# Attention over grouped heads beside a quantized feed-forward: two runs of transposes and one score product are put into one row inside a projection

## The reference

```python
q = (x @ wq).reshape(B, S, 32, 128)      # 32 query heads
k = (x @ wk).reshape(B, S, 8, 128)       # 8 key and value heads, 4 query heads to each
v = (x @ wv).reshape(B, S, 8, 128)
q, k = rope(q), rope(k)
scores = einsum('bqhgd,bshd->bhgqs', qg, k) * 128 ** -0.5
allowed = (j <= i) & (j > i - 128)       # a sliding window of 128 positions
attn = softmax(where(allowed, scores, most_negative))
out = einsum('bhgqs,bshd->bqhgd', attn, v).reshape(B, S, 32 * 128) @ wo
h = silu(xn @ W1.T) * (xn @ W3.T);  ffn = h @ W2.T   # W1, W3, W2 from packed 4-bit numbers
```

## Time and profile before

| | |
|---|---|
| median of 3 runs | 802.33 us (802.15 to 803.08) |
| profiled execution | 802.26 us |
| its span, first to last instruction | 800.4 us |
| granted TensorE clock over the span | 1.000 of full speed |
| TensorE matrix products busy | 796.0 us (99%) |
| VectorE, ScalarE, GpSimd busy | 567.4, 428.5, 475.2 us |

### The profile page before, as it was taken

The page is one execution under the profiler, slowest core; times in us unless marked ns, Lnnn a source line. Parts: engine busy times, 40 slices in busy tenths (PEclk is TensorE's granted clock), DMA queues, the critical chain, the costliest instruction groups (busy, mean ns, idle before and its releaser), DMA issues.

```text
span 800.4 us, 13468 instructions
## 1 busy us (share of the span) xinstructions
PE 796.0 (99%) x3966; PEld 672.4 (84%) x3966; DVE 567.4 (71%) x1634; ACT 428.5 (54%) x1104; POOL 475.2 (59%) x357
## 2 busy tenths in 40 slices
PE   9999999999999999999999999999999999999998
PEld 7888888888888888888888888888888888888887
DVE  7715867668448867767686777778677777867785
ACT  5413313223138675666666566666656566665672
POOL 2103314224256774867487486748757674878997
PEclk9999999999999999999999999999999999999999
DMA  9659525201000400400040040004004000420102
GB/s 282 187 178 269 139 67 158 77 29 53 1 27 14 132 14 1 132 2 14 2 131 13 0 131 0 13 0 131 13 0 131 0 13 0 131 66 0 40 0 106
DMA packets 51908, 54.00 MB, mean 67 GB/s; under 512 B 4128, under 2 KB 33184, under 8 KB 51872
## 3 DMA queue, kind: packets, MB, share of 16 engines
q1 hardware_dynamic: 51728, 53.50, 22.6%
q10 hardware_dynamic: 144, 0.07, 0.0%
HBM read 47.25 MB, written 6.29 MB: 67 GB/s over the span
## 4 chain that ended last, share of the span: by engine, by line
PE 93%; POOL 4%; issue 2%; ACT 0%; DVE 0%; POOLq 0%; ACTq 0%
PE bank L1349 26%; PE bank L1350 26%; PE bank L1351 26%; PE bank L1540 3%; PE bank L1556 3%; PE bank L1573 2%; PE bank L1574 2%; PE bank L1575 2%; PE bank L1582 1%; POOL swap L457 1%; PE bank L1579 1%; PE bank L1580 1%; PE bank L1478 1%; POOL acc L488 1%; POOL q L461 1%
## 5 line engine op out<-in xcount | busy, mean ns | idle before, releaser
L457 POOL TENSOR_TENSOR swap<-swap,cst 128x512 f32<-128x512 f32 x80 | 107.9, 1349 | 41.7 <-ACT swap L701 41.7
L722 ACT ACTIVATE probs<-probs,nmx 128x128 f32<-128x128 f32 x256 | 100.0, 392 | 59.9 <-DVE nmx L1123 59.8
L1349 PE MATMUL bank<-xh,wih 128*128 128x512 f32 x320 | 128.9, 403 | 0.0
L1350 PE MATMUL bank<-xl,wih 128*128 128x512 f32 x320 | 125.2, 391 | 0.0
L1351 PE MATMUL bank<-xh,wil 128*128 128x512 f32 x320 | 125.0, 391 | 0.0
L1349 PE MATMUL bank<-woh,oh 128*128 128x512 f32 (+1 forms) x260 | 100.9, 388 | 0.0
L1350 PE MATMUL bank<-wol,oh 128*128 128x512 f32 (+1 forms) x260 | 100.6, 387 | 0.0
L1351 PE MATMUL bank<-woh,ol 128*128 128x512 f32 (+1 forms) x260 | 100.5, 387 | 0.0
L405 POOL TENSOR_TENSOR hl<-act_h,hh 128x512 fp32r<-128x512 f32 x22 | 31.6, 1436 | 99.6 <-ACT hh L603 99.6
L461 POOL TENSOR_TENSOR q<-q,swap 128x512 f32<-128x512 f32 x64 | 86.0, 1344 | 6.6 <-DVE q L1098 1.6
L480 POOL TENSOR_TENSOR ph<-ph,cst 128x512 fp32r<-128x512 f32 x32 | 41.8, 1305 | 73.3 <-ACT ph L737 73.3
(11 more groups left out here) (140 smaller groups left out, 2026.9 us busy)
## 6 DMA issues: line engine op xcount, KB each, us to landing
raw<-in_wq SPq DMA_DIRECT2D x32, 256.0 KB, 4.6
raw<-in_wo SPq DMA_DIRECT2D x32, 256.0 KB, 5.0
pk<-in_w SPq DMA_DIRECT2D x44, 128.0 KB, 3.6
sc<-in_s SPq DMA_DIRECT2D x44, 128.0 KB, 3.8
vals<-stage SPq DMA_DIRECT2D x16, 256.0 KB, 2.8
vraw<-vals SPq DMA_DIRECT2D x16, 256.0 KB, 2.9
pk<-in_w SPq DMA_DIRECT2D x11, 256.0 KB, 2.7
sc<-in_s SPq DMA_DIRECT2D x11, 256.0 KB, 3.1
```

The lines of the kernel that those rows point to most:

```text
L457: nc.gpsimd.tensor_tensor(v, v, spread(sin.unsqueeze(1), P, 2, SEQ), ALU.mult).then_inc(sin_done, 1)
L722: e = nc.scalar.activation(probs[:, s, c0:c1], probs[:, s, c0:c1], ACT.Exp, bias=nmx[:, s, i:i + 1], scale=-1.0, accum_out=rsum[:, s, i:i ...
L1349: nc.tensor.matmul(out_, sh, mh, start=(i == 0), stop=False)
L1350: nc.tensor.matmul(out_, sh, ml, start=False, stop=False)
```

## The change

In a step's list of TensorE, three pieces of plain fp32 work stood apart: the four transposes of the second batch's first blocks before chunk 1 of the fifth projection (c = 4), the four of its second blocks before chunk 2, and the first score product of the next step behind the projection. Now all three stand together before chunk 1: eight transposes, then the score product with its plain and its split part, and chunks 1 to 3 of the projection after them. `first_step` and the lists of the other engines are as they were.

```diff
                 out_project(g, bp, 0)
-                project(ng, nbp, 4, {1: lambda: p_turn(g, bp, 1, 0), 2: lambda: p_turn(g, bp, 1, 1)})
-                scores(ng, nbp, 0, 0)
+                def plain_ones():
+                    p_turn(g, bp, 1, 0)
+                    p_turn(g, bp, 1, 1)
+                    scores(ng, nbp, 0, 0)
+
+                project(ng, nbp, 4, {1: plain_ones})
                 attend(g, bp, 1)
                 scores(ng, nbp, 0, 1)
```

## The result

The changed kernel takes 810.04 us (810.0 to 810.33, 6 runs) against 802.28 us of the kernel before (6 runs): a ratio of 1.0096, with a 95% interval from 1.0086 to 1.0107. It is slower by 7.8 us. The forecast was 809.4 us, with a range of 808.2 to 810.6.

The account below looks back on a forecast made before the run. TensorE was taken as the bound, with no slack at the output projection's wait. Thirteen steps at 0.54 us gave 7.0 us, plus 0.1 for the last: 7.1 over 802.26, so 809.4 us, range 808.2 to 810.6.

Parts of the forecast that it names:

- where the slack is zero: Output projection t = 1 waits for the low part of attention output 2; its load starts 0.05 to 0.06 us behind.
- rival A: At the output projection the 0.05 us is chance and nothing waits: 801.9 us, not slower; chance 0.07.
- The saving: TensorE's list from first transpose to `attend` gets shorter at its edges: 0.03 us a step, bounds 0 and 0.07.
- D: Delay of the fifth projection's last product by the score block in front: 0.54 us a step, 7.0 us for thirteen.
- The chain is rigid: From the projection's last product through ScalarE's copies and high parts to VectorE's low part: all links 0.54 us later, length unchanged.
- Rival B: At the output projection the weight load hides in the longer wait: 0.43 us a step, 808.0 us; chance 0.05.
- The cover of 0.30 us: At the score product: time left between its query's low part (L1105) and the split part's first load; no wait expected.
- rival C: A second wait, at the score product for its query's low part, in seven steps: 2.1 us more, 811.5 us; chance 0.04.
- the forecast's 0.16: Fourteenth step, (7,0): low part ends at 768.05 against 767.89, so 0.16 us later instead of 0.54; bounds 0 and 0.54.

Follow-up runs that it names:

- e3: Changed kernel with output projection t = 1 writing another bank, so needing only attention output tiles 0 and 1: 801.91 us, ratio 0.9995.
- e6: Kernel before with ScalarE's high part of attention output 2 put before the high part of query 3: 802.10 us, ratio 0.9996.
- e7: Kernel before with the eight transposes in one row and output projection t = 1 in the other bank: 801.68 us, ratio 0.9990.
- e4: Changed kernel with ScalarE's high part of attention output 2 put before the high part of query 3: 805.61 us, ratio 1.0041.
- e2: Kernel before with only the score product moved, to before chunk 3 of the fifth projection, transposes left apart: 809.71 us, ratio 1.0092.
- e1: Kernel before with only the eight transposes in one row before chunk 1, score product left behind the projection: 801.80 us, ratio 0.9995.

## Why the prediction was right

- What bounds the kernel, and where the slack is zero: right. The load 0.05 us behind one and the same releaser was no chance (rival A). e3 and e6 show both sides of it: without the wait the order of the change costs nothing, and with 0.2 us of slack a step of the kernel before is only 0.02 us shorter. That the wait cost "nothing visible" was right for the total, which e6 doesn't tell from no change.
- The saving: forecast 0.03 us a step. Measured are 0.00 up to `attend` (3.54 us in both) and 0.01 in a step without the wait (e7 against e6); in the changed kernel the wait takes that too. The nine products take 415.88 - 413.79 = 2.09 us, not 9 x 0.23 = 2.07, and the block takes 0.58, not 0.57. My 3.51 us summed spacings rounded to 0.01 us. The edges were free in the kernel before: its first product behind four transposes starts 0.36 us behind the first of them (410.27 to 410.63), not 0.44, and the next one 0.31 us later (410.94), not 0.23, which is the same 0.67 us in sum.
- The cost, D: forecast 0.54 us, measured 0.57 at the projection's last product (3.30 less 2.74, 0.573 unrounded) and 0.58 in a step. The term missed by the saving that wasn't there. The last 0.01 us of a step lies behind the wait: the ten products from the third of the output projection on take 2.293 us in the mean of the thirteen steps, against 2.285 before. Thirteen steps gave 7.56 us where 7.0 were forecast; this is nearly all of the difference to 810.04.
- The chain is rigid: right. e4 took a link of 0.32 us out of it and got 0.30 a step, and e2 moved its start by the block alone.
- Rival B, the load hidden in the longer wait: it did not happen. The second product of the output projection starts at 419.32, 0.39 us behind the low part's end at 418.92, the distance of before. The load starts behind the release, at 418.98, and so it does in all fourteen steps, 0.05 us behind the low part's end. The Trainium skill, "TensorE: Matmul & The Clock Gate", section "Step-by-step: what each phase is for", tells of loads pulled ahead of products in flight. At these fourteen waits the load isn't pulled ahead of the wait in front of it.
- The cover of 0.30 us at the score product held in the thirteen steps. It failed in the fourteenth, (7,0), for which the forecast had not worked it out. There, in the trace after, all engines:

```profile
769.73 1.00 DVE L1105 TENSOR_TENSOR ql<-q,qh 128x256 fp32r<-128x256 f32 x1
...
770.24 0.39 PE L1540 MATMUL bank<-k,q 128*128 128x128 f32 x2
...
770.78 0.19 PEld L1349 LDWEIGHTS bank<-kh,qh 128*128 128x128 f32 x1 [0.35 <-DVE ql L1105]
770.79 0.38 PE L1349 MATMUL bank<-kh,qh 128*128 128x256 f32 x1 [0.16 <-DVE ql L1105]
```

TensorE waits for the low part of the query there, and the split part starts 0.55 us behind the plain one, not 0.14. So rival C's mechanism did occur, once. The output projection's second product was 0.6 us late, 0.39 us of it by this wait (`attend` starts 3.93 us behind the first transpose, not 3.54); the forecast had 0.16 us in all, entered into its sum as 0.1. But the next step's first transpose came 785.48 - 769.37 = 16.11 us behind this one's, against 777.41 - 761.50 = 15.91 us before. That is 0.20 us for the step. It is near the forecast's 0.16 by luck, since it is the difference of two larger terms that the forecast didn't have: 0.6 us lost and 0.4 us given back. What gave it back stands in the kernel before, in its trace of PEld and then of PE, from the first of a pair of score products to the output projection behind it:

```profile
773.28 0.30 PEld L1540 LDWEIGHTS bank<-k,q 128*128 128x128 f32 x2 [0.21 <-DVE nmx L1123]
```

```profile
773.34 0.43 PE L1540 MATMUL bank<-k,q 128*128 128x128 f32 x2
...
774.73 0.40 PE L1349 MATMUL bank<-woh,oh 128*128 128x512 f32 x1
```

The same pair in the trace after:

```profile
781.79 0.38 PE L1540 MATMUL bank<-k,q 128*128 128x128 f32 x2
...
782.94 0.40 PE L1349 MATMUL bank<-woh,oh 128*128 128x512 f32 x1
```

It takes 1.39 us before and 1.15 us after. Before, the load of its first score product waits for VectorE's masking (L1123); after, it doesn't. The next pair gives back 0.14 us more (1.29 us before, 1.15 after).

Why the query's low part came late in this one step stays open, but the experiments narrow it down. In the changed kernel it ends 1.36 us behind the first transpose. In e3 and e4, which have the same list of TensorE, it ends at 0.47 and 0.20 us, and no such wait appears. In e2 it ends at 1.36 us too, but the score product's split part stands at 2.42 us and needn't wait. So the place of the score product doesn't make the low part late. The two kernels in which it is late are the two with a step of 35.70 us; what in that length does it was not tried. e2 is also the better test of the forecast's 0.16 us: without the wait for the query its output projection's load starts 0.20 us later in this step than in the kernel before (6.64 against 6.44 us behind the first transpose).

The sum by the profiles: 7.56 us for the thirteen steps, and 0.20 for the fourteenth. That makes 7.76 us, which is the difference of the medians. The profiled executions are 810.33 and 802.26 us, 8.07 apart; the other 0.31 us lie before 305 us, where the two programs are the same. Among the eight kernels here the first transpose of (0,1) starts between 304.9 and 305.7 us, so this part differs from one profile to the next by as much.

## What to carry to other kernels

On an engine that is busy all the time and waits for next to nothing, moving its work around was worth no more here than its edges, 0.01 us a step, and it cost a whole block, 0.58 us a step: ask for each item that is moved forward which result it now stands in front of, and who waits for that. A busy share of 100% can hide waits with no slack, here 0.02 us a step in the kernel before; look for an instruction that starts at the same small distance behind the same releaser in every repetition. Where a wait comes from a shared buffer and not from data, another buffer can take it away: e3 got the whole 7.8 us back with one changed bank.

## What was not expected of the hardware

Behind the wait the products stand a little wider apart. From the start of the output projection's third product to that of the sixth it takes 0.680 us in e3, e6 and e7, in the mean of the thirteen steps, where TensorE isn't held in front of it. It takes 0.694 us in the kernel before, where TensorE is held by 0.02 us, and 0.695 us in the changed kernel. Why was not tried.

The nine products behind the score block took 0.232 us each in the mean (413.79 to 415.88), above the 0.227 us (0.680 / 3) of those undisturbed ones; why is not known either. The row of eight transposes passes into the plain score product without any extra time (0.87 us from the first transpose to L1540, the 0.87 us of eight). Putting the transposes together saved 0.01 us a step (e1, and e7 against e6), so a change between the two kinds of product costs next to nothing here.
